# Full attention's scores from exact high and low parts instead of four-pass float32

## What is computed

```python
qkv = x @ wi.T + bi
q, k, v = jnp.split(qkv, 3, axis=-1)          # 16 heads of width 16
scores = jnp.einsum('bhqd,bhkd->bhqk', q, k) / jnp.sqrt(hd)
attn = jax.nn.softmax(scores, axis=-1)
o = jnp.einsum('bhqk,bhkd->bhqd', attn, v)
x = _layernorm(x + o @ wo.T + bo, ln1_g, ln1_b)
```

## Time and profile before

| | us |
|---|---|
| median of 3 runs | 2404.18 (2403.26 to 2404.22) |
| profiled execution, its own time | 2391.44 |
| its span, first to last instruction | 2389.6 |
| busy: PE / DVE / ACT / POOL | 2039.4 / 1524.2 / 1161.6 / 1065.4 |
| first score matmul of stage three | at 1430.20 |
| first turned score (slot 0 of period 0) | at 1492.37 |
| exponentials of period 0 / 1 / 6 / 7 begin | 1494.49 / 1573.20 / 1969.68 / 2044.47 |

### The profile page before, as it was taken

One profiled execution on the slowest core, in us unless ns is written; L12 is line 12 of the kernel. 1 busy time (PEld: TensorE's weight loads), 2 busy tenths in 40 slices (PEclk: granted clock), 3 DMA queues, 4 the chain that ended last, 5 costly groups with the idle time before them and its releaser, 6 DMA issues.

```text
span 2389.6 us, 33476 instructions
## 1 busy us (share of the span) xinstructions
PE 2039.4 (85%) x11408; PEld 1095.2 (46%) x11408; DVE 1524.2 (64%) x3278; ACT 1161.6 (49%) x2719; POOL 1065.4 (45%) x840
## 2 busy tenths in 40 slices
PE   7999999999899999875768966989999998864996
PEld 4555555555555555542336842323333332222664
DVE  4348687677868686849834537656766666253665
ACT  5676666766666766631112430455555545530121
POOL 2017475665847484845745522102222111045675
PEclk9999999999999999987889987999999999986999
DMA  8224533434100000041234732111111150212222
GB/s 289 80 72 169 180 135 116 142 111 147 58 24 5 15 5 14 1 135 32 89 131 144 218 98 78 31 43 46 39 53 51 46 179 16 67 36 93 80 84 69
DMA packets 175729, 204.59 MB, mean 86 GB/s; under 512 B 19305, under 2 KB 157417, under 8 KB 175306
## 3 DMA queue, kind: packets, MB, share of 16 engines
q1 hardware_dynamic: 124442, 121.75, 16.0%
q0 software_dynamic: 16752, 45.84, 6.3%
q10 hardware_dynamic: 34368, 34.87, 4.3%
HBM read 83.75 MB, written 114.46 MB: 83 GB/s over the span
## 4 chain that ended last, share of the span: by engine, by line
PE 56%; DVE 15%; POOL 9%; ACT 9%; issue 6%; another core or an unknown queue 2%; DMA 2%; SPq 1%; POOLq 0%; DVEq 0%; ACTq 0%
PE ps L1887 11%; POOL prod L853 8%; ACT m_pt L2046 6%; PE ps L580 3%; PE ps L607 3%; PE ps L566 3%; DVE pb L735 3%; PE ps L591 3%; PE ps L617 3%; DVE sc L865 3%; PE ps L1901 3%; PE ps L2256 3%; PE ps L2248 2%; PE ps L1309 2%; PE ps L1845 2%
## 5 line engine op out<-in xcount | busy, mean ns | idle before, releaser
L1978 DVE TENSOR_REDUCE m_mx<-ps 128x2 f32<-128x1024 f32 x256 | 311.6, 1224 | 172.0 <-PE ps L1866 170.0
L735 DVE CUSTOM_DVE_ANT_0 pb<-ps,bias,snl 128x128 f32<-128x128 f32 (+3 forms) x512 | 260.4, 547 | 226.5 <-PE ps L580 225.2
L2046 ACT ACTIVATE m_pt<-ps 128x1024 f32<-128x1024 f32 x256 | 260.2, 1023 | 289.2 <-PE ps L1887 289.2
L853 POOL TENSOR_TENSOR prod<-qs,kvs 128x1024 f32<-128x1024 f32 x120 | 283.9, 2393 | 163.5 <-issue 142.3
L853 POOL TENSOR_TENSOR prod<-sc,kvs 128x1024 f32<-128x1024 f32 x120 | 280.4, 2369 | 98.6 <-ACT sc L971 85.8
L1887 PE MATMUL ps<-m_q,m_k 32*128 32x512 f32 x1024 | 274.1, 647 | 50.7 <-ACT m_pt L2046 39.8
L931 ACT ACTIVATE pb<-pb,mst 128x129 f32<-128x129 f32 (+3 forms) x512 | 283.5, 560 | 19.1 <-DVE mst L735 17.1
L1866 PE MATMUL ps<-m_k,m_q 32*128 32x512 f32 x1024 | 276.2, 660 | 9.0 <-DVE m_mx L1978 8.0
L580 PE MATMUL ps<-kz,qT 64*128 64x128 f32 (+3 forms) x1024 | 186.0, 442 | 0.0
L2065 POOL DMA_INDIRECT m_yg<-ye_scratch,e_pos x64 | 63.1, 987 | 270.2 <-DVE m_x L1966 232.9
L591 PE MATMUL ps<-ident,pb 128*128 128x128 f32 x1280 | 179.3, 279 | 0.5 <-DVE mst L735 0.4
(11 more groups left out here) (329 smaller groups left out, 3790.5 us busy)
## 6 DMA issues: line engine op xcount, KB each, us to landing
xh_scratch<-zt SPq DMA_DIRECT2D x43, 768.0 KB, 8.5
xe_scratch<-zt ACTq DMA_DIRECT2D x32, 1024.0 KB, 4.8
ye_scratch<-e_ys SPq DMA_DIRECT2D x36, 256.0 KB
hw_w<-in_w SPq DMA_DIRECT2D x16, 512.0 KB, 6.2
xin<-in_x SPq DMA_DIRECT2D x8, 512.0 KB
y_scratch<-e_y SPq DMA_DIRECT2D x8, 512.0 KB
m_x<-y_scratch SPq DMA_DIRECT2D x8, 512.0 KB, 4.1
x1c_scratch<-e_x SPq DMA_DIRECT2D x8, 512.0 KB
```

The source lines that it names most:

```text
L735: dv.tensor_tensor_reduce(pb.ap[:, j, SEG[t]:SEG[t] + n], rS.of(("S", b, p, t, j)).ap[:, 0:n], k.bias[:, h, CAUSAL[t]:CAUSAL[t + 1]], -1.0 ...
L853: e.tensor_tensor(out, one, two, ALU.mult).then_inc(*k.c.did(*product_done(step, b, t, u)))
L1978: dv.tensor_reduce(x.ap[:, t, 64 * half:64 * half + 64].rearrange("p (i r) -> p i r", i=2)[:, :, 16], score_ring(k, b).of((b, g, t, half)) ...
L2046: ac.activation(p.ap[:, 2 * half:2 * half + 2, :], k.qE.of((b, g, kt, half)).ap, ACT.Exp).then_inc(*did("m_exp", b, g, kt, half))
```

## The change

The scores are computed from operands in float32r, a float32 whose mantissa is cut short. To lose nothing, q and k are split into a high part that such an operand holds exactly and the exact rest.

- `p_qk` projects half a group at a time (256 columns, two steps a group). ACT writes each half twice: rounded into `m_qa` (float32r, the high parts) and in full into a single scratch cell `m_zq`. With the second half POOL subtracts `m_qa` from `m_zq` twice, into `m_kb` and `m_qb` (128x512 each, L2126 and L2128), and SP makes twelve transfers of 16 rows where it made four, waiting before the last four for the first four to land.
- A score is then two matmuls (high against both parts, low against both parts), the turned one has a third: minus the maximum, from the new cells `m_M` against a constant `m_one`. The new function `scores` issues them in rounds: in each of the first two rounds two turned and two straight matmuls, then the third, turned pair alone. It waits for everything that both need before its first matmul.
- `m_neg` no longer changes q on DVE. POOL splits the maxima into two parts (new step `m_split`, two small operations, slot 2 of each group), PE turns them (slot 5 of each group), and ACT copies them into `m_M`.
- `p_v` is four steps of one tile instead of two of two.
- The tables of slots are new, and batch 1's gathers and blends are spread: two gathers stand between the projections of batch 0, the rest and all blends in period -1, between the first maxima.
- The 12 fills of `m_k` with ones on ACT become one small one; one fill pair on DVE is gone; buffers are laid out anew, and the early loads of the next stage (`h_load`) come in two parts.

```diff
-    return {4: [("p_x", b)], 6: [("p_gather", b, 0)], 8: [("p_gather", b, 1)], 11: [("p_blend", b, 0)],
-            12: [("p_gather", b, 2)], 14: [("p_blend", b, 1)], 15: [("p_gather", b, 3)], 18: [("p_blend", b, 2)],
-            22: [("p_blend", b, 3)], 23: [("p_keep", b)]}
-TURN, QK, VAL, FT, FO = (0, 1), (4, 6, 8, 12), (14, 16), (13, 15, 21, 23), (20, 22, 28, 30)
+    return {18: [("p_x", b)], 20: [("p_gather", b, 0)], 22: [("p_gather", b, 1)], 25: [("p_blend", b, 0)],
+            26: [("p_gather", b, 2)], 28: [("p_blend", b, 1)], 29: [("p_gather", b, 3)], 32: [("p_blend", b, 2)],
+            36: [("p_blend", b, 3)], 37: [("p_keep", b)]}
+TURN, QK, VAL = (15, 17), ((18, 20), (24, 26), (32, 34), (40, 42)), (36, 38, 44, 46)
+FT, FO = (7, 9, 23, 25), (16, 22, 28, 30)
...
-        if s % 8 == 2 and 0 <= n + 24 < 32 * NB:
-            out[s].append(("m_neg", (n + 24) // 32, (n + 24) % 32 // 8))
+        if s % 8 == 2 and 0 <= n + 22 < 32 * NB:
+            out[s].append(("m_split", (n + 22) // 32, (n + 22) % 32 // 8))
+        if s % 8 == 5 and 0 <= n + 19 < 32 * NB:
+            out[s].append(("m_neg", (n + 19) // 32, (n + 19) % 32 // 8))
...
-    out += [("p_qk", 0, g) for g in range(G4)] + [("p_v", 0, 0), ("p_v", 0, 1)] + first(1)
+    out += [("p_x", 1), ("p_qk", 0, 0, 0), ("p_qk", 0, 0, 1), ("p_gather", 1, 0), ("p_qk", 0, 1, 0), ("p_qk", 0, 1, 1), ("p_gather", 1, 1)]
+    out += [("p_qk", 0, g, i) for g in (2, 3) for i in range(2)] + [("p_v", 0, t) for t in range(NT)]
...
+            w.wait_ge(at("m_qkc", b, g, 1), at("m_kl", b, g), at("m_ql", b, g))
             for j in range(4):
-                sp.dma_start(u.ap[32 * j:32 * j + 16, :], q.ap[32 * j + 16:32 * j + 32, :]).then_inc(*did(f"d_k{u.i}", b, g, j))
+                sp.dma_start(bits(kb)[low[j], :], bits(qa)[high[j], :]).then_inc(*did(f"d_kh{kb.i}", b, g, j))
+            for j in range(4):
+                sp.dma_start(bits(qb)[high[j], :], bits(qa)[low[j], :]).then_inc(*did(f"d_qh{qb.i}", b, g, j))
+            w.wait_ge(at(f"d_kh{kb.i}", b, g, 3))
+            for j in range(4):
+                sp.dma_start(bits(qa)[high[j], :], bits(qb)[low[j], :]).then_inc(*did(f"d_ql{qa.i}", b, g, j))
...
+def scores(k, pe, w, tops, turned):
+    did, last = k.c.did, {}
+    for b, g, t, half in turned:
+        w.wait_ge(at("m_less", b, g), at("m_one", 0), k.qE.take((b, g, t, half), at("m_exp", b, g, t, half)).room)
...
+    for p, ring in enumerate((k.qa, k.qb)):
+        for b, g, t, half in turned:
+            m, q, kb = k.qE.of((b, g, t, half)), ring.of((b, g)), k.kb.of((b, g))
+            for i in range(2):
+                j = 2 * half + i
+                pe.matmul(m.ap[:, i, :], band(kb.ap, j)[:, t * P:(t + 1) * P], band(q.ap, j), start=(p == 0), stop=False,
+                          tile_position=(32 * j, 0))
+        for b, g, t, half in tops:
...
+    for b, g, t, half in turned:
+        m, less = k.qE.of((b, g, t, half)), k.mM.of((b, g))
+        for i in range(2):
+            j = 2 * half + i
+            x = pe.matmul(m.ap[:, i, :], band(k.mone, j), band(less.ap, j), start=False, stop=True, tile_position=(32 * j, 0))
+        x.then_inc(*did("m_ST", b, g, t, half))
...
+        elif step == "p_qk" and key[2]:
...
+            po.tensor_tensor(kb.ap[:, :], z.ap[:, :], bits(qa), ALU.subtract).then_inc(*did("m_kl", b, g))
+            w.wait_ge(qb.room)
+            po.tensor_tensor(qb.ap[:, :], z.ap[:, :], bits(qa), ALU.subtract).then_inc(*did("m_ql", b, g))
```

216 lines of the change are left out of this document (123 added, 93 removed).

## The result

The changed kernel takes 2378.96 us (median of 5, 2367.75 to 2385.49) against 2403.26 of the kernel before in the same comparison, a ratio of 0.9901 with a 95% interval of 0.9873 to 0.9929. It is faster, by 24 us or 1.0%; the forecast was 2352, 52 us faster. The experiments ran on five chips: on four of them the kernel before takes 2351.66 to 2354.5, on the fifth (only the run with the weights on ACT's queue) 2388.24. The changed kernel was run again on one of the four, where its ratio is 0.9886 (0.9867 to 0.9905). So experiments are compared by their ratios, and traces by the lengths of stretches, not by the times at which things happen.

A forecast was written before the change was run, and what follows sets the result against it. Bound: mostly a 2.25 us slot loop of turned scores and exponentials through one PSUM cell, PE where steps are added. Terms sum to -52 on 2391.4: 2339 profiled, median 12.7 above, 2352; range 2328 to 2380 (own 2340 to 2366).

The forecast's parts named there:

- period 5, without gathers behind slot 20, 71.4: Stage three, period 5: with no gathers behind slot 20 it would take 71.4 us, -7.9 in the sum.
- rival 4: POOL's subtractions take about 1.9 each beside DVE's work, at the start and in each wait: 2366 to 2372; chance 0.07.
- The new wait: Middle periods: SP's twelve transfers delay `f_load`, then POOL, DVE and PE; 2.9 a period, about 0.9 more in slots after.
- Rival 1: SP's and POOL's queues don't collide, as both run ahead enough; another 4 x 3.5 less: 2338; chance 0.17.
- A pass: PE's score matmuls: a float32r matmul is one pass of 0.213 us, making the slot loop 2.04 instead of 2.25.
- The weight loads: PE's weight loads of score rounds 2 and 3 were taken as hidden beside matmuls, costing nothing.
- Rival 2: PE's weight loads in rounds 2 and 3 show, 0.22 to 0.38 a slot: 2401 to 2437; chance 0.10.
- The start: Before period 0: POOL becomes the chain, first maximum near 1438.5, first turned score near 1485: -7 (-3 to -14).
- The clock: PE stalls of over 2 us may bring its clock down a window: +2 in the sum.

The follow-up runs named there:

- the second run: The changed kernel, unedited, run again beside the kernel before on one of the four chips of the experiments: ratio 0.9886 (0.9867 to 0.9905).

## Why the prediction was wrong, point by point

**The step that failed** is the term "period 5, without gathers behind slot 20, 71.4". It counted what period 5 lacks, the gathers, and left out what stands in it alone: 16 loads of 512 KB and one of 2 MB on the very queue on which the forecast's wait hangs. It took 86.3. That is 14.9 of the 28 us by which the sum was off, and the runs show it whole: with the loads spread period 5 is 73.4, with `f_load` early 72.7, with both 71.3. The loads were in the trace of before too and cost nothing there, though POOL's bias step waited for `m_z` in the same way (1947.53); the change put the split of the maxima, and so PE, behind that step. With the time of 2378.96 the range of 2328 to 2380 was still met, but by luck: its upper end stood for rival 4, which didn't happen, and the forecast's own 2340 to 2366 was missed.

**The new wait** was right, in mechanism and nearly in size: 4.58 for slot 31 against 4.94 forecast; all of it together 3.5 a period on the first chip (74.8 on average less 71.3), 4.5 on the chip of the second run, against 3.9. Two experiments confirm the links: early `f_load` removes it, and eight copies fewer remove it from slot 31, though there a new wait comes out in slot 29. Part of the near hit is luck, as two links missed in opposite directions. Counted from slot 20's start in period 1, SP is through its twelve copies at 13.7 (forecast 12.9; issues start 0.63 apart, not 0.6), while the split takes 0.6 instead of 1.2, and the power ends at 27.7 (27.2). Rival 1 (the queues don't collide) fell.

**A pass** was right: one record for a float32r matmul, loads hidden. A round came out at 0.23 instead of 0.213 (the slot without the third one is 0.23 shorter), so the loop is 2.08 and not 2.04, and slots with four transposes 2.48 and not 2.43. That is 1.3 us a period, about 9 in seven of them: the second largest miss. Period 0's first slot adds 1.5 (3.59, with a granted clock of 0.5 up to 1494.0) and slot 31 of period 6 0.6 (2.65), which about accounts for the misses of these two periods.

**The weight loads.** Rival 2 fell: the load of a round (1565.53 to 1565.72) runs beside the matmul of its own band (1565.42 to 1565.91), and the next round starts at 1565.76. The Trainium skill, "TensorE: Matmul & The Clock Gate", Part 3 (what overlaps and what doesn't), lets a load overlap with matmuls in flight only where the row group differs, and would have had these loads wait; for float32r as for float32 the trace disagrees. **Rival 4** fell: a subtraction on POOL takes 1.28 beside DVE's maxima, as taken. What was missed there is the opposite direction, POOL holding up DVE: in the changed kernel as it stands one blend a period takes 0.85 instead of 0.48. It does so with both edits too, where the slots around it are 2.08, so that costs nothing.

**The start** was right within 0.8, and so were its parts. Counted from the first projection: first score 20.9 (forecast 21.3), first maximum 22.1 (21.3), first turned score 67.8 (67.8). Behind the first maximum stand maxima of 37.3 (36.3), twelve blends of 6.1 (6) and 3.3 of waits for PE (4), at a mean granted clock of 0.65. One reading was wrong without harm: the 16 records in 9.63 of the earlier trace rows are at half clock only at first; they start 0.85 apart up to 1421.6 and 0.43 apart from 1422.4 on.

**The clock.** The sum had +2 for it. Of periods 1 to 6 it fell only in period 5, to 0.5 in PE's wait of 11.2, and one slot shows it, by 0.8; PE's waits of 2.6 in periods 1 to 4 left it at 1.00.

**The ends.** The stage began 3.6 us later in the first trace, and the last stages took 4.3 more. The second was -2.3 where both kernels were run again. The first is not clear: in all twelve traces of the changed kernel and its variants on the four chips of 2352, stage three is reached 2.7 to 9.4 us later than in the one trace of the kernel before there, though the change doesn't touch the stages ahead of it. Some of that is there within the first 90 us and differs from run to run; 2.0 to 2.6 of it comes in between 1222 and 1314 in each of the twelve, but on the first chip only 0.4. With one trace of the kernel before to compare with, it stays open.

With period 5 at its 71.4 the profiled run would have been at 2353, and the median near 2364, still 12 above the forecast: the round, period 0's first slot and the two ends.

## What to carry to other kernels

When a change makes one engine's queue the critical one, list everything that is issued on that queue in each repetition of the loop, one-off loads of the next stage above all, and look at how many bytes each moves: the one period that differs can take back the gain of two others. A load that someone will wait for belongs ahead of a burst of issues, not behind it; here moving two of them by twelve or thirteen slots gave more (30 us) than the whole change (27). And an edit that "undoes" an order also moves the loads in it past other queues' work: keep them in place, or the run measures them.

## What the runs showed of the hardware

- **DVE and POOL hold each other up on SBUF operands.** A blend on DVE (two SBUF inputs) took 2.50 instead of 0.48 beside two POOL subtractions, a POOL subtraction 1.76 instead of 1.28 behind a DVE one that started 0.05 earlier, while maxima read from PSUM kept their 1.23. The Trainium skill, "SBUF — State Buffer", section "SBUF: two separate sides", says that the two share a port pair as an exclusive lock held for the whole instruction, also for a DVE instruction with two SBUF inputs against a POOL one that reads SBUF; by that rule it is a wait and not a slowdown. The numbers fit that but for 0.2: the blend ends 0.29 behind POOL's second subtraction (alone it takes 0.48), and the POOL subtraction ends 1.13 behind DVE's (alone it takes 1.28).
- **The price of an operand's type.** Four matmuls of 512 columns side by side take 0.23 in float32r and 0.86 in float32, in two programs that differ in the type alone.
- **A small load behind large ones.** 128 KB land in 1.7 to 2.3 us on a free queue, in 6.3 to 6.8 directly behind 2 MB on the same one, and in the kernel before, where weight loads stood directly ahead of the 2 MB, 13.1 passed from the issue until its reader started.
- **SP's issues.** Copies of 16 rows start 0.63 apart on SP's queue, so twelve of them hold it for 7.6 us.
- **Chips differ.** The kernel before took 2351.66 to 2354.5 on four chips, 2388.24 on a fifth and 2403.26 in the first comparison; its two traces, from the first comparison and from one of the four, both have periods of 79.3.
